# A selective scan with a quantised layer: three PSUM banks for the scans' inputs, one for everything else, and a new order of all engines

## The reference, cut to what matters

```python
def s6(x, A_log, D, x_proj_w, dt_proj_w, dt_proj_b):      # x: 8 x 2048 x 512, 16 states
    A = -jnp.exp(A_log)
    xp = jnp.einsum('bld,ed->ble', x, x_proj_w)
    d_rank, Bm, Cm = xp[..., :64], xp[..., 64:80], xp[..., 80:]
    delta = jax.nn.softplus(jnp.einsum('blr,dr->bld', d_rank, dt_proj_w) + dt_proj_b)
    # for each step t, h is d x n:  h = exp(delta*A)*h + delta*Bm*x ;  y = sum_n h*Cm
    return ys + x * D

def ffn(x, weight_q, weight_scale, bias):
    x_scale = jnp.maximum(jnp.max(jnp.abs(x), -1, keepdims=True), 1e-6) / 127.0
    x_q = jnp.clip(jnp.round(x / x_scale), -128, 127).astype(jnp.int8)
    return (x_q @ weight_q.T) * x_scale * weight_scale + bias

x = x + s6(layernorm(x), ...)
x = x + ffn(layernorm(x), ...)
```

## Time and profile before

| | |
|---|---|
| median of 3 runs | 2882.73 us |
| the profiled execution | 2883.35 us, its span 2881.6 |
| TensorE matmul, weight load, busy | 2827.7 us (98%), 2540.2 (88%) |
| VectorE, ScalarE, GpSimd, busy | 2763.0 (96%), 2741.2 (95%), 2765.2 (96%) |
| granted TensorE clock, mean | 0.995 of full speed |
| DMA | 321 MB, 111 GB/s on average |

### The profile page before, as it was taken

How to read it: one execution, slowest core, us unless ns; L and a number is a source line. 1 busy time by engine, 2 the same in 40 slices (tenths; PEclk the granted TensorE clock), 3 DMA queues, 4 the chain that set the end, 5 groups by cost and what they waited for, 6 DMA issues and landing times. The chain is left out here.

```text
span 2881.6 us, 59680 instructions
## 1 busy us (share of the span) xinstructions
PE 2827.7 (98%) x22782; PEld 2540.2 (88%) x22844; DVE 2763.0 (96%) x2766; ACT 2741.2 (95%) x4990; POOL 2765.2 (96%) x1040
## 2 busy tenths in 40 slices
PE   8999999999999999999999999999999999999997
PEld 6888899888999898998888888989989898988885
DVE  6999999999999999999999999999999999999996
ACT  8999999999999999999999999999999999999993
POOL 4899999999999999999999999999999999999997
PEclk9999999999999999999999999999999999999998
DMA  5344435354343444353544434443434444343333
GB/s 199 103 119 122 105 91 128 101 122 118 100 115 105 124 122 109 87 131 98 122 115 103 115 99 131 122 101 96 121 109 122 115 103 115 103 127 93 86 81 81
DMA packets 198368, 321.23 MB, mean 111 GB/s; under 512 B 93057, under 2 KB 93057, under 8 KB 181698
## 3 DMA queue, kind: packets, MB, share of 16 engines
q1 hardware_dynamic: 164242, 250.29, 27.4%
q0 software_dynamic: 33840, 67.11, 15.0%
HBM read 212.70 MB, written 104.66 MB: 110 GB/s over the span
## 5 line engine op out<-in xcount | busy, mean ns | idle before, releaser
L473 POOL TENSOR_TENSOR A<-A,CB 128x2048 f32<-128x2048 f32 x511 | 2364.4, 4821 | 39.0 <-ACT CAR L538 38.5
L799 DVE TENSOR_TENSOR_SCAN A<-A,CAR,PB 128x512 f32<-128x512 f32 x1536 | 1866.2, 1264 | 43.4 <-PE PB L663 16.0
L531 ACT ACTIVATE A<-DEL,an 128x512 f32<-128x512 f32 x2048 | 1364.9, 715 | 0.4
L688 PE MATMUL Y<-idf,A 128*128 128x128 f32 x8192 | 1139.1, 273 | 1.3 <-DVE A L853 1.3
L553 ACT ACTIVATE DB<-XN,BC 128x512 f32<-128x512 f32 x1408 | 962.5, 714 | 0.1
L688 PEld LDWEIGHTS Y<-idf,A 128*128 128x128 f32 x8192 | 943.5, 141 | 8.2 <-DVE A L853 1.8
L666 PE MATMUL PB<-idf,DB 128*128 128x128 f32 x5632 | 847.7, 275 | 11.5 <-DVE A L799 6.2
L666 PEld LDWEIGHTS PB<-idf,DB 128*128 128x128 f32 x5632 | 651.7, 141 | 121.8 <-issue 70.1
L663 PEld LDWEIGHTS PB<-DG,XN 128*128 128x128 f32 x5120 | 631.6, 192 | 92.4 <-issue 70.7
L663 PE MATMUL PB<-DG,XN 128*128 128x128 f32 x5120 | 679.2, 277 | 14.4 <-DMA DG<-b_diag 5.2
L799 DVE TENSOR_TENSOR_SCAN A<-A,PB 128x512 f32<-128x512 f32 x512 | 598.5, 1207 | 30.6 <-PE PB L663 15.8
(11 more groups left out here) (87 smaller groups left out, 1700.1 us busy)
## 6 DMA issues: line engine op xcount, KB each, us to landing
CB<-c_rows SPq DMA_DIRECT2D x128, 1024.0 KB, 4.9
DG<-b_diag SPq DMA_DIRECT2D x160, 256.0 KB, 5.3
out<-bib SPq DMA_DIRECT2D x32, 1024.0 KB, 6.2
out<-X POOLq DMA_DIRECT2D x32, 1024.0 KB, 9.8
X<-in_x SPq DMA_DIRECT2D x31, 1024.0 KB, 5.7
out<-C POOLq DMA_DIRECT2D x31, 1024.0 KB, 9.4
b_diag<-DG SPq DMA_DIRECT2D x2, 1280.0 KB, 12.8
b_diag<-BC SPq DMA_DIRECT2D x160, 2.0 KB, 5.8
```

The costliest lines, as they stand in the source:

```text
L473: gp.tensor_tensor(A[s % NA][:, :, :], A[s % NA][:, :, :], CB[:, s % (4 * NG), :].unsqueeze(1).broadcast_to([128, KB, L]), ALU.mult).then_ ...
L531: act.activation(A[s % NA][:, g, :], DEL[k % 2][:, g, :], ACT.Exp, scale=an[:, g, n:n + 1])\
L688: i = pe.matmul(Y[j][:, g * 128:(g + 1) * 128], A[s % NA][:, g, j * 128:(j + 1) * 128], idf[:, :], is_transpose=True, start=False, stop=(n ...
L799: dve.tensor_tensor_scan(A[s % NA][:, g, :], A[s % NA][:, g, :], PB[(4 * s + g) % 2][:, :], init, ALU.mult, ALU.add).then_inc(s_scan, 1)
```

## The change

It does five things. (1) PB has three banks: fill u waits for scan u - 3. (2) PQ is gone; q_t and q_mm use PM, in turn with x_t, x_p, b_c, d_t and dl_t. For that x_t of chunk p waits for scale_a of chunk p - 3, and q_t of chunk p for du of chunk p + 2. (3) GpSimd multiplies all four pieces of the last unit; `last_c` is gone. (4) TensorE transposes the identity 56 times in the tail, in four groups, each behind a semaphore of the last chunk's chain. (5) All places are new. The diff, without the tables and without edits that only put in NV = 0:

```diff
-        PB = [ps(f"PB{i}", [128, L]) for i in range(2)]
+        PB = [ps(f"PB{i}", [128, L]) for i in range(NPB)]   # NPB = 3
...
-        PQ = ps("PQ", [128, 512])
...
         def bank_q(p, j):
-            return PQ if p < NCH - 1 else Y[j]
+            return PM if p < END else Y[j]
...
             def times_c(k, n):
                 if s == NS * NCH - 1:
-                    for g in range(KB - 1):
+                    for g in range(KB):
...
             def tb(k, i):
                 u = 4 * s + g
-                if u >= 2:
-                    pe.wait_ge(s_scan, u - 1)
+                if u >= NPB:
+                    pe.wait_ge(s_scan, u - NPB + 1)
...
+            def idle(p, i):
+
+                if p == END:
+                    if i == 0:
+                        pe.wait_ge(s_y, T * NCH)
+                        pe.wait_ge(s_oa, T * END)
+                    elif i == 1:
+                        pe.wait_ge(s_sq, T * NCH)
+                    elif i == 2:
+                        pe.wait_ge(s_as, NCH)
+                    else:
+                        pe.wait_ge(s_k, NCH)
+                    for _ in range((16, 22, 12, 6)[i]):
+                        pe.transpose(PM[:, 0:128], idf[:, :], idf[:, :])
...
             def x_t(p, g):
                 if g == 0:
+                    if p >= 3:
+                        pe.wait_ge(s_oa, T * (p - 2))
...
             def q_t(p, j):
-                if j == 0 and p >= 1:
-                    pe.wait_ge(s_oa, (T - NV) * p)
+                if j == 0:
+                    pe.wait_ge(s_du, T * min(p + 3, NCH))
+                    if p >= 1:
+                        pe.wait_ge(s_oa, T * p)
...
-            def last_c(p):
```

More of the change, by code:

```diff
@@ L48 @@
[L48 to L52, removed]
[8 rows of a table removed]
[L61 to L68, removed]
+        "act_b": (-100, -98, -52, -43, -26, -22, -3, -2, 1, 76, 141, 164, 170, 179, 200, 203, 233, 253, 275,
@@ new lines @@
+        "gather": (1182, 1192, 1239, 1252),
+        "idle": (1896, 1906, 1916, 1926),
+        "last_q": (-42, 474, 633, 751),
+        "load": (-2136,),
+        "load_c": (-133, 68, 190, 191),
+        "load_g": (-374, -272, -231, 10, 17),
+        "put_bias": (839,),
+        "q_mm": (2076, 2113, 2147, 2162),
+        "q_t": (1936, 1968, 2006, 2023),
+        "qt_out": (1950, 1983, 1999, 2025),
+        "rstd0": (-1203,),
+        "scale_a": (2071, 2155, 2166, 2196),
+        "scale_out": (1587, 1614, 1773, 2056),
@@ L69 @@
+        "step": (1431,),
+        "store_c": (-424,),
+        "store_g": (-468,),
[8 rows of a table added]
+        "times_c": (-113, 78, 317, 322, 331, 354, 366, 423, 544, 561, 612, 645, 671, 695, 811, 875),
+        "var1": (1443,),
+        "weights": (-1910,),
+        "x_p": (-586, -581, -567, -566),
+        "x_t": (-818, -733, -667, -615),
+        "xn": (-963, -918, -896, -841),
+        "xp_out": (-515,),
+        "xt_out": (-754, -692, -618, -587),
 }
 FIRST = {
-        "act_b": (-679, -675, -643, -544, -540, -503, -475, -371, -341, -318, -193, -138),
@@ L73 @@
[L73 to L84, removed]
-        "load_g": (-2300, -1939, -1845, -1812, -1674),
@@ L98 @@
-        "xt_out": (-5386, -4953, -4868, -4454),
+        "act_b": (-434, -432, -365, -315, -314, -312, -236, -184, -142, -115, -93, -28),
+        "aggr0": (-2830,),
+        "b_c": (-1143,),
+        "bc_out": (-683,),
+        "carry": (-43, 162),
+        "d_t": (-2105, -1363, -1361, -1195),
+        "decay": (-467, -340, -263, -168, -148, -133, -120, -112, -103, 29, 29, 42),
+        "delta": (-1867, -1551, -1062, -886),
+        "dl_t": (-1035, -1019, -942, -877),
+        "du": (-1700, -1396, -1219, -1011),
@@ new lines @@
+        "eps0": (-3996,),
+        "load": (-4332,),
+        "load_c": (-570, -118, 62, 286),
+        "load_g": (-1190, -778, -437, -240, -16),
+        "rstd0": (-5217,),
+        "scan": (-299, -284, -180, -178, -168, -168, -168, -54),
+        "stats0": (-3884, -3857, -3787, -3461),
+        "store_c": (-3379,),
+        "store_g": (-3047,),
+        "tb": (-456, -453, -423, -359, -305, -162, -146, -121),
+        "th": (158, 190, 195, 197),
+        "times_c": (-69, 89),
+        "x_p": (-3190, -3000, -2392, -2256),
@@ L111 @@
-        "q_t": (1829, 2140, 3268, 3990),
-        "qt_out": (5660, 5667, 5831, 6081),
-        "scale_a": (2736, 3339, 3514, 4186),
-        "scale_out": (6935, 7006, 7310, 7500),
-        "scale_p": (3070, 3880, 4173, 4915),
-        "scales": (4294,),
-        "square": (1309, 1443, 1597, 1759),
-        "step": (4625,),
-        "var1": (2394,),
+        "add_c": (5760,),
+        "add_x": (4263,),
+        "amax": (3051,),
+        "ascale": (4852,),
+        "centre": (3623, 4136, 5544, 6412),
@@ new lines @@
+        "gather": (2110, 2236, 2825, 2895),
+        "idle": (3044, 3054, 3064, 3074),
+        "last_q": (4219, 4508, 4662, 4711),
+        "put_bias": (355,),
+        "q_mm": (4179, 4949, 4998, 5057),
+        "q_t": (3084, 3591, 3610, 3705),
+        "qt_out": (3795, 4027, 4064, 4136),
+        "scale_a": (5694, 5819, 6596, 7057),
+        "scale_out": (4911, 5232, 5284, 5576),
+        "scale_p": (5633, 5674, 6044, 6475),
+        "scales": (3769,),
+        "square": (1919, 1944, 2000, 2742),
@@ L120 @@
+        "step": (5039,),
+        "var1": (3024,),
 }
@@ L774, in q_mm @@
                 i.then_inc(s_mm, 1)
-            run(x_t=x_t, x_p=x_p, d_t=d_t, b_c=lambda p, i: b_c(p), dl_t=dl_t, q_t=q_t, q_mm=q_mm, tb=tb, th=th)
+            run(idle=idle, x_t=x_t, x_p=x_p, d_t=d_t, b_c=lambda p, i: b_c(p), dl_t=dl_t, q_t=q_t, q_mm=q_mm, tb=tb, th=th)
         @block.vector
```

134 lines of the change are left out of this document (46 added, 88 removed), and 16 rows, old and new, of the table PLACES.

## The result

The changed kernel takes 2846.41 us, the median of 4 runs, against 2883.09 us for the kernel before in the same comparison: a ratio of 0.987 (0.9851 to 0.9889), or 36.7 us less. The prediction said 2864, 19 us less. The execution that was profiled first had a mean granted clock of 0.85 and took 3202.33 us, so all rows here are from a repeat of the same kernel (2845.73 us, span 2844.0).

What follows compares the result with a forecast made beforehand. It took TensorE (86.3 of 88.0 us per chunk) and VectorE, catching each other's unevenness, as the bound. 2883.35 - 18.6 (third bank) + 1.9 (head) - 1.9 (idle transposes) = 2864.75, stated as 2864 us; range 2846 to 2896.

Steps and rivals of the forecast that it cites:

- What bounds the kernel: Whole chunk: TensorE fullest, 86.3 of 88.0 us; TensorE and VectorE, near their limits, catch each other's unevenness.
- Third PB bank: Scan fills in each chunk: half of VectorE's 1.17 us PB waits go, 0.6 us per chunk, -18.6 us in all.
- One bank for projections and quantised rows: q_t and q_mm sharing PM in each chunk: cost at nothing, at worst 1.1 us per chunk.
- Order of the accumulating DMA: Squares overwriting C after its transfer out: 1 us of room left, costed at nothing.
- Head: Weights' cast before du in chunk 0: du 2.9 us later, +1.9 us in all (0 to +4).
- Last product: Tail, all four pieces on GpSimd: product ends 1.7 us sooner, but gain in the end 0.
- Idle transposes: Tail, 56 transposes keep TensorE's clock up so the four last transfers go back to back: -1.9 us.
- (a): Rival: the third bank's room is used in full, period 86.9 us, 2847 us; chance 0.14.
- (b): Rival: nothing moves, TensorE is the bound and loses time to other waits, period 88.0, 2883 us; chance 0.16.
- (c): Rival: slower, the shared bank stalls TensorE at q_mm 2 behind scale_a 1, 2902 us; chance 0.23.

Runs made afterwards that it cites:

- less_pool: Changed kernel with scale_p on 8 columns instead of 512 on GpSimd, leaving weight scales out of the output: 2830.87 us, ratio 0.9804.
- vector_scale_2: Changed kernel with VectorE scaling each chunk's first output quarter, scale_p 1 behind times_c 1, and the weights' cast behind du: 2833.11 us, ratio 0.9815.
- before_less_pe: Kernel before the change without the one-row matmul ahead of each q_t on TensorE, rounding left out: 2855.98 us, ratio 0.9899.
- less_pe: Changed kernel without the one-row matmul ahead of each q_t on TensorE, rounding left out: 2844.15 us, ratio 0.9849.
- order_only: Changed kernel with two PB banks and a separate PQ for q_t and q_mm, without the two sharing waits: 3102.91 us, ratio 1.076.
- two_banks: Changed kernel with two PB banks instead of three, PM still shared, all else as changed: 3103.28 us, ratio 1.0761.
- cast_late: Changed kernel with the cast of the weights put back behind du: 2844.67 us, ratio 0.9868.
- last_on_dve: Changed kernel with the last quarter of the last product given back to VectorE: 2849.16 us, ratio 0.988.
- no_idle: Changed kernel without the 56 idle transposes in the tail: 2847.68 us, ratio 0.9878.

## Why the prediction was right and wrong

**What bounds the kernel** was right for the kernel before: TensorE, 86.3 us of work by its sum. Its wall shows at 86.5 in `less_pool` and `vector_scale_2`, and `before_less_pe` shows that it was the one that counted most. What the section did not do is add up the second engine. GpSimd's own sum could be had from the same trace, 88.04 less the 1.33 us that it waits: 86.7. With TensorE at 86.3 to 86.5 and GpSimd at 86.7 to 86.9, the first wall below the old period of 88.0 stood 1.2 us under it, and it was GpSimd's.

**Third PB bank: the term that was mis-sized.** The step says "I take half, 0.6 us". Measured for bank, sharing and order together: 1.16, the far end of the step's own bounds (1.17 us, period "86.9"; measured 86.88). The reason for the half was that TensorE "would then still idle 1.1 us per chunk, for the waits that have nothing to do with PB". It does not. By the prediction's own sum of 86.3 it idles 0.6. Its weight loads' waits for a free bank, 1.03 us per chunk, went to 0.03; what is left are waits for GpSimd's products, 4.2 / 23 = 0.2 for matmuls and 0.4 for weight loads. No row stands behind the half: of waits "that have nothing to do with PB" the matmuls' rows of the kernel before hold only 3.2 + 2.3 us, 0.24 per chunk, and those went as well. The row that the bounds came from was also the wrong one. VectorE's PB waits were to be halved and grew, from 26.6 to 35.7 us in 2000; VectorE has room, so its waits say little. Those that count are TensorE's for a free bank and GpSimd's for ScalarE. The two fit one chain (TensorE late, scan late, carry late, product late), and ScalarE's own waits for scans fell with them, from 13.3 to 0.2; that they are one chain is argued, not shown by a run. The gain stopped where GpSimd has no more to give, as `less_pool` and `less_pe` show. (1.16 - 0.6) x 31 = 17 us, nearly all of the miss.

**One bank for projections and quantised rows: right.** "Cost at nothing": `order_only` and `two_banks` are 0.4 us apart, and in the changed kernel, with three banks PB, TensorE waits for no other engine at any user of PM between 500 and 2500 us. Around q_mm 2 of chunk 16 (the third group of q_mm on TensorE) nothing waits:

```profile
1431.12 0.81 PE L784 MATMUL PM<-wqb,QT 128*128 128x512 bf16 x3
1431.77 1.04 PE L682 MATMUL Y<-idf,A 128*128 128x128 f32 x8
1432.64 1.04 PE L660 MATMUL PB<-idf,DB 128*128 128x128 f32 x8
```

It was close there. scale_a 1 ended at 1430.4, 3.6 us after carry 1's scan and not 2.7; TensorE reached q_mm 2 at 1430.8 all the same, because it was not as far ahead as its banks allowed. The price depends on the order: in the old one sharing and the places it forces cost 6.4 us per chunk or more.

**Order of the accumulating DMA: right.** The transfer out of C is issued at 1439.3 and lands 9.0 us later, at 1448.3; the first square is at 1450.7. There are 2.4 us of room, the prediction had 1. No square waits between 500 and 2500 us.

**Head: its own step right, its sum too small a view.** du starts at 27.64, 2.5 us later than before (28.1 and 2.9 said), and the first scan 3.0 us later, with three more pieces of statistics ahead of it. `cast_late` prices the cast at 1.7 us, the prediction at 1.6. But the step then forecast a loss of 1.9 in all, and by chunk 2 the kernel is 4.1 us ahead. Twelve scans in a row follow, and TensorE's half clock ends at 35.6 us instead of 45.1. "VectorE is the full engine of chunk 0" took its statistics as moved, not its waits for TensorE as gone. Whether bank, order or clock did this was not separated.

**Last product: the mechanism half right, the end too low.** Four pieces on GpSimd take 5.21 us (4.95 said), and none is slower than VectorE's quarter was (6.75 us). "Gain in the end: 0" is not borne out in the changed kernel: with VectorE's quarter the span is 4.0 us longer, the median 3.5, though the ratios' intervals overlap, and part of it is the clock. Nor does scale_a 3 start "when it does now": it starts 11.8 us after the last scan (2817.7), where the kernel before had 8.8, mainly since GpSimd began its pieces later. What the edit alone would have given in the kernel before, where GpSimd began with VectorE, was not run. The Trainium skill's rule ("Trainium Architecture — The Big Picture", "The five engines, in one table") of GpSimd streaming about two times slower would have made this edit a loss. By `last_on_dve` the trace does not agree: beside GpSimd's own products VectorE's quarter ended at 2815.89, where GpSimd's fourth piece ends at 2808.63 + 5.21 = 2813.84 in the changed kernel.

**Idle transposes: right.** The clock stays at 1.00, the one-row matmul is at 2826.90, and the four transfers are 3.61 us together, back to back from the landing. -1.9 said; `no_idle` puts 1.9 between the last issues, by the mechanism that was named. What was not foreseen is that GpSimd, now the wall, trails the scans by 2.7 us when they end (last scan 2805.9, last product 2808.63; before, 2844.4 and 2844.48), which is why the time from last scan to end grew by 0.9.

**Rivals.** (a) named the period (86.9) and the time (2847) but held VectorE's waits for the measure; the runs give another mechanism. (b) falls with the period. (c) falls with the rows of the changed kernel: scale_a 1 does end more than 1.6 us after carry 1's scan, as its condition asks, but TensorE does not wait at q_mm 2. `order_only` agrees, though only with two banks.

## What to carry to other kernels

Where all engines are above 95%, add up the work of every one and not only of the fullest: the second wall, not a share of some wait, tells how much an edit can give. Read the waits of the fullest engine for its buffers; those of an engine with room may grow while the kernel gets faster. An order written by hand is made for its number of buffers (8.2 us per chunk lost by taking one away), so buffers and order are tried together. Afterwards the walls are looked up again, since work can now move from the new one.

## What the runs showed of the hardware that was not expected

- A VectorE product with two SBUF inputs (128x512, fp32) took 9.65 us in `last_on_dve`. It was issued while one GpSimd product ran and 2.65 us ahead of the five that followed, which came at 1.2 us each, (2812.57 - 2808.89) / 3. It ended 0.56 us after the last of these (2812.57 + 2.76 = 2815.33). In the kernel before it took 6.75 us beside such a row and ended at 2851.18, 0.55 us after GpSimd's fifth product; a sixth, begun 0.06 us after the fifth, took 1.62 us where the others took 1.25 to 1.27. The Trainium skill, "SBUF — State Buffer", "Who interferes with whom", says that a VectorE instruction with two SBUF inputs contends with a GpSimd one that reads SBUF, and that issue order decides who blocks. The trace agrees that it blocks, but not that the one issued first goes first once GpSimd's current instruction is over: in `last_on_dve` three pieces and two more products that came later were through before it.
